# Graph network, kernel for one core: softmax weights and x1 are split into float16 halves before they are transposed, and the halves are transposed by DMA

## What is computed

```python
x = _layernorm(x + _L0_gnn_ref(x, adj, ...))     # two layers of graph attention
x = _layernorm(x + _L1_gnn_ref(x, adj, adj, ...))

# L0, for l in 0, 1
u = (u_left * (upper triangle and diagonal) + u_right * (lower triangle)) of adj   # u_* = h (h W_*)^T / sqrt(384)
delta = exp(u) * adj
h = relu(layer_norm(delta / (sum(delta) + 1e-10) @ (h W_lin^T + b_lin)) )

# L1, 12 heads of 32
scores = q k^T * 384 ** -0.5 + 2 * adj
p = softmax(scores), rows that are all zero give 0
out = (p @ v) W_o^T + b_o
```

## Time and profile before

| | |
|---|---|
| median of 3 runs | 2787.72 us |
| profiled execution | 2789.46 us |
| its span, first to last instruction | 2787.6 us |
| mean granted clock of TensorE | 0.992 of full speed |
| busy: PE, DVE, ACT, POOL | 98%, 85%, 66%, 53% |
| 16 DMA engines, queue of SP | 11.6% |

### The profile page before, as it was taken

One profiled execution on the slowest core, in us unless ns is written; L12 is line 12 of the kernel. 1 busy time (PEld: TensorE's weight loads), 2 busy tenths in 40 slices (PEclk: granted clock), 3 DMA queues, 4 the chain that ended last, 5 costly groups with the idle time before them and its releaser, 6 DMA issues.

```text
span 2787.6 us, 74097 instructions
## 1 busy us (share of the span) xinstructions
PE 2736.2 (98%) x27072; PEld 1766.4 (63%) x27072; DVE 2375.9 (85%) x8170; ACT 1846.2 (66%) x4363; POOL 1472.2 (53%) x1558
## 2 busy tenths in 40 slices
PE   6999999999999999999999999999999999999996
PEld 3666666666666666666666666666666666666664
DVE  4788988889888889888888888898888898888986
ACT  4666676666776666766666766667666667666665
POOL 2555464455555554654555554556545556445553
PEclk9999999999999999999999999999999999999998
DMA  4001101011101011010111010111011110101000
GB/s 169 23 34 49 46 22 46 34 49 46 49 22 46 35 49 46 25 43 35 49 49 46 22 46 35 49 46 37 31 37 46 49 46 22 46 35 49 25 28 18
DMA packets 55993, 116.68 MB, mean 42 GB/s; under 512 B 4945, under 2 KB 37713, under 8 KB 55633
## 3 DMA queue, kind: packets, MB, share of 16 engines
q1 hardware_dynamic: 55632, 111.96, 11.6%
HBM read 86.77 MB, written 25.17 MB: 40 GB/s over the span
## 4 chain that ended last, share of the span: by engine, by line
PE 97%; DVE 1%; issue 1%; ACT 0%; DMA 0%; POOL 0%; SPq 0%; POOLq 0%; DVEq 0%; ACTq 0%
PE psum L1243 72%; PE psum L1253 11%; PE psum L1307 7%; PE psum L1402 4%; PE psum L1376 3%; DMA s<-weights 0%; DVE s L837 0%; DVE y L900 0%; DVE st L962 0%; DVE z L1014 0%; DVE st L908 0%; DVE o L881 0%; DVE pT_lo L802 0%; ACT w L583 0%; DVE z L1023 0%
## 5 line engine op out<-in xcount | busy, mean ns | idle before, releaser
L583 ACT ACTIVATE w<-s,nmax 128x128 f32<-128x128 f32 x1536 | 480.6, 393 | 2.4 <-DVE nmax L837 2.4
L1243 PE MATMUL psum<-hT_hi,w_hi 128*128 128x512 f16 x1152 | 439.3, 381 | 12.1 <-POOL hT_lo L378 11.9
L459 POOL TENSOR_TENSOR fold<-s 128x768 f32<-128x768 f32 x128 | 242.2, 1892 | 387.5 <-DVE nmax L837 285.5
L1243 PE MATMUL psum<-hT_hi,w_lo 128*128 128x512 f16 x1152 | 438.1, 380 | 0.0
L1243 PE MATMUL psum<-hT_lo,w_hi 128*128 128x512 f16 x1152 | 438.1, 380 | 0.0
L523 ACT ACTIVATE nT_hi<-psum 128x512 f16<-128x512 f32 x384 | 227.5, 594 | 300.1 <-PE psum L1243 298.1
L837 DVE CUSTOM_DVE_ANT_0 s<-psum,adj 128x128 f32<-128x128 f32 x1536 | 339.4, 285 | 6.1 <-DVE live L857 0.5
L386 POOL TENSOR_TENSOR hl_lo<-hl_raw,hl_hi 128x384 fp32r<-128x384 f32 x256 | 238.6, 952 | 103.5 <-ACT hl_hi L523 99.2
L804 DVE SCALAR_TENSOR_TENSOR nT_lo<-psum,nT_hi 128x512 f16<-128x512 f32 x384 | 258.3, 683 | 31.0 <-ACT nT_hi L523 31.0
L802 DVE TENSOR_TENSOR pT_lo<-psum,pT_hi 128x512 f16<-128x512 f32 x384 | 251.2, 683 | 25.9 <-ACT pT_hi L523 25.5
L523 ACT ACTIVATE pT_hi<-psum 128x512 f16<-128x512 f32 x384 | 214.6, 594 | 81.4 <-PE psum L1253 80.6
(11 more groups left out here) (135 smaller groups left out, 7942.0 us busy)
## 6 DMA issues: line engine op xcount, KB each, us to landing
xTin<-xT SPq DMA_DIRECT2D x32, 768.0 KB, 4.8
xres<-x SPq DMA_DIRECT2D x32, 768.0 KB, 4.4
out<-y SPq DMA_DIRECT2D x128, 192.0 KB, 1.9
adjm<-adjM SPq DMA_DIRECT2D x32, 384.0 KB, 5.4
adjT_sb<-adjT SPq DMA_DIRECT2D x32, 256.0 KB, 5.5
adj<-adj SPq DMA_DIRECT2D x32, 256.0 KB, 2.8
x<-weights SPq DMA_DIRECT2D x4, 576.0 KB, 4.6
s<-weights SPq DMA_DIRECT2D x3, 576.0 KB, 6.4
```

Source lines behind the costliest of these rows:

```text
L459: nc.gpsimd.tensor_tensor(fold[:, :, 0:n], src[:, :, 0:n], src[:, :, n:2 * n], ALU.add)\
L583: last = nc.scalar.activation(w[:, m], s[b % 2][:, m], ACT.Exp, bias=nmax[b % 2][:, m:m + 1], scale=-1.0)
L1243: last = mm(dst, a, b, start=(i == 0), stop=(i == total - 1))
```

## The change

1. x1 and w are split where they lie, in the layout of tokens by features. ACT writes x1_hi (4 copies of 384) and p_hi (3 copies of 512 per graph). DVE writes x1_lo and two of three parts of p_lo, POOL the third. x1_hi and x1_lo lie in the buffer of xTin, p_hi and p_lo in the buffer s of the same graph.
2. PE's transposes x1t and pt are gone. SP issues `dma_start_transpose` for each half: two for x1 (turn_x) and two for each graph's weights (turn_p), ten a pass, of 128 x 1536 float16 each.
3. Waits: qk(0) and v(0) wait for both transfers of x1, pv(b) for both of its graph; DVE's scores(b, 0) waits until the transfers that read the same s are done; ACT's exps wait for pt_lo and pt_end (POOL's part) in place of PE; the load of the next xTin waits for the transfers of x1; out_bias on POOL waits for x1_lo.
4. xT_hi and xT_lo are laid out graph first.
5. All orders are new: BANK_USES, and `body` of SP, POOL, ACT, DVE and PE. Among them: PE does ctx(0, 0) and ctx(0, 1) ahead of qk(0); u(0) ahead of hl(0, 2); DVE does x1's low halves ahead of u(0, 0); xt(0) to xt(2) follow qk(3) on ACT; pv(1), pv(2) and v(3) come later.

The core of the diff:

```diff
-        xT_hi, xT_lo = (sb(f"xT_{p}", [KB, GROUP, TOK], f16) for p in ("hi", "lo"))
+        xT_hi, xT_lo = (sb(f"xT_{p}", [GROUP, KB, TOK], f16) for p in ("hi", "lo"))
...
+        def halves(buf, n):
+
+            all16 = buf.bitcast(f16)
+            return [all16[:, h * n:(h + 1) * n] for h in range(2)]
+
+        x1_hi, x1_lo = halves(xTin[:].rearrange("p k b t -> p (k b t)"), GROUP * FEAT)
+        p_hi, p_lo = zip(*(halves(b[:].rearrange("p h t -> p (h t)"), HEADS * TOK) for b in s))
...
+            def turn_x(p):
+
+                if not p.l1:
+                    return
+                if p.before.l1:
+                    sp.wait_ge(qk_full.sem, p.before.upto(qk_full, 2 * KB))
+                    sp.wait_ge(v_full.sem, p.before.upto(v_full, GROUP))
+                for ok, src, dst in ((x1t_hi, x1_hi, xT_hi), (x1t_lo, x1_lo, xT_lo)):
+                    sp.wait_ge(ok.sem, p.upto(ok, GROUP))
+                    sp.dma_start_transpose(dst[:].rearrange("p b k t -> p (b k) t"), src).then_inc(xT_in.sem, 16)
+
+            def turn_p(p, b):
+
+                if not p.l1:
+                    return
+                if b >= 2:
+                    sp.wait_ge(pv_full.sem, p.upto(pv_full, b - 1))
+                elif p.before.l1:
+                    sp.wait_ge(pv_full.sem, p.before.upto(pv_full, b + 3))
+                sp.wait_ge(pt_hi.sem, p.upto(pt_hi, KB * (b + 1)))
+                sp.dma_start_transpose(pT_hi[b % 2][:], p_hi[b % 2]).then_inc(pT_in[b % 2].sem, 16)
+                sp.wait_ge(pt_lo.sem, p.upto(pt_lo, 2 * (b + 1)))
+                sp.wait_ge(pt_end.sem, p.upto(pt_end, b + 1))
+                sp.dma_start_transpose(pT_lo[b % 2][:], p_lo[b % 2]).then_inc(pT_in[b % 2].sem, 16)
...
+                turn_x(p)
+                load_adj(p)
+                load_x(p)
+                load_adjT(p)
+                load_tri(p)
+                store(p, 2)
+                turn_p(p, 0)
+                turn_p(p, 1)
+                store(p, 3)
+                load_res(p)
+                turn_p(p, 2)
+                store(p, 0)
+                turn_p(p, 3)
+                store(p, 1)
...
+            def pt(p, b, r):
+
+                if not p.l1:
+                    return
+                pool.wait_ge(p_ok.sem, p.upto(p_ok, TILES * (b + 1)))
+                pool.wait_ge(pt_hi.sem, p.upto(pt_hi, KB * b + r + 1))
+                part = slice(TILES * r * TOK, TILES * (r + 1) * TOK)
+                nc.gpsimd.tensor_tensor(p_lo[b % 2][:, part], w[:].rearrange("p h t -> p (h t)")[:, part],
+                                        p_hi[b % 2][:, part], ALU.subtract).then_inc(pt_end.sem, 1)
...
             def pt(p, b, r):
                 if not p.l1:
                     return
...
-                hi(p, pt_full, KB * b + r, "pt", pT_hi[b % 2][:, TILES * r:TILES * (r + 1)], pt_hi)
+                act.wait_ge(fold1.sem, p.upto(fold1, b + 1))
+                act.wait_ge(p_ok.sem, p.upto(p_ok, TILES * b + r + 2))
+                part = slice(TILES * r * TOK, TILES * (r + 1) * TOK)
+                copy(p_hi[b % 2][:, part], w[:].rearrange("p h t -> p (h t)")[:, part]).then_inc(pt_hi.sem, 1)
...
+                of, n = (p, b - 2) if b >= 2 else (p.before, b + 2)
+                if j == 0 and of.l1:
+                    dve.wait_ge(live_ok.sem, of.upto(live_ok, n + 1))
+                    dve.wait_ge(pT_in[b % 2].sem, of.upto(pT_in[b % 2], 32 * (n // 2 + 1)))
...
-            def pt(p, b, r):
-
-                if not p.l1:
-                    return
-                n = KB * b + r
-                p.await_bank(pe, "pt", n)
-                pe.wait_ge(p_ok.sem, p.upto(p_ok, TILES * b + r + 2))
-                turn("pt", n, [w[:, TILES * r + i] for i in range(TILES)], pt_full)
-
...
-                pe.wait_ge(pt_lo.sem, p.upto(pt_lo, (b + 1) * KB))
+                pe.wait_ge(pT_in[b % 2].sem, p.upto(pT_in[b % 2], 32 * (b // 2 + 1)))
```

More of the change, by code:

```diff
@@ L299, in store @@
                     .then_inc(out_st[b % 2].sem, 16)
-            def body(p):
[L302 to L328, removed]
@@ new lines, in load_adj, with load_x @@
+            def load_adj(p):
+                if not p.l1:
+                    return
+                if p.before.l1:
+                    sp.wait_ge(s_ok.sem, p.before.upto(s_ok, GROUP * TILES))
+                sp.dma_start(adj2[:], adj[bass.ds(p.it - 1, 1)].rearrange("g i b j -> i (g b) j"))\
+                    .then_inc(adj2_in.sem, 16)
+            def load_x(p):
+                if not p.nxt:
+                    return
+                sp.wait_ge(xt_hi.sem, xt_hi.upto(p.it, KB))
+                sp.wait_ge(xt_lo.sem, xt_lo.upto(p.it, KB))
+                if p.l1:
+                    sp.wait_ge(xT_in.sem, p.upto(xT_in, 32))
+                sp.dma_start(xTin[:], xT[bass.ds(p.it + 1, 1)].rearrange("g p k b t -> p (g k) b t"))\
+                    .then_inc(x_in.sem, 16)
@@ new lines, in load_tri, with load_adjT @@
+            def load_tri(p):
+                if not p.nxt:
+                    return
+                sp.wait_ge(mask_ok.sem, mask_ok.upto(p.it, 1))
+                sp.dma_start(adjm[:], adjM[bass.ds(p.it + 1, 1)].rearrange("g j b c -> j (g b) c"))\
+                    .then_inc(adj_in.sem, 16)
+            def load_adjT(p):
+                if not p.nxt:
+                    return
+                if p.before.l0:
+                    sp.wait_ge(e_ok[1].sem, p.before.upto(e_ok[1], 2))
+                sp.dma_start(adjT_sb[:, 1 - p.odd], adjT[bass.ds(p.it + 1, 1)].rearrange("g j b i -> j (g b) i"))\
+                    .then_inc(adjT_in.sem, 16)
@@ L700, in body @@
                 ctx(p, 0, 3)
+                fin(p, 2)
+                qk(p, 0)
+                qk(p, 1)
                 qk(p, 2)
                 qk(p, 3)
+                fin(p, 3)
+                xt(p, 0)
+                xt(p, 1)
+                xt(p, 2)
                 qk(p, 4)
@@ L720, in body @@
                 nl(p, 1, 1)
-                v(p, 1)
+                exps(p, 1, 0)
                 exps(p, 1, 1)
-                nl(p, 1, 2)
                 exps(p, 1, 2)
-                v(p, 2)
+                pt(p, 1, 0)
+                setup(p, 8)
                 exps(p, 1, 3)
[L727 to L734, removed]
@@ L735, in body @@
-                fin(p, 3)
                 pt(p, 1, 1)
                 pt(p, 1, 2)
+                setup(p, 9)
+                hl(p, 1, 0)
+                v(p, 0)
+                v(p, 1)
                 exps(p, 2, 0)
+                nl(p, 1, 2)
+                nl(p, 1, 3)
+                v(p, 2)
                 exps(p, 2, 1)
                 exps(p, 2, 2)
+                exps(p, 2, 3)
+                pt(p, 2, 0)
+                pt(p, 2, 1)
+                to(p, 0)
+                hl(p, 1, 1)
@@ L1102, in body @@
                 resid(p, 3)
-                setup(p, 4)
-                y_bn(p, 1)
-                nl(p, 0, 4)
-                nl(p, 0, 5)
                 y_bn(p, 2)
@@ L1347, in qk @@
                 w = slice(kb * 128, (kb + 1) * 128)
-                product(bank("qk", c), [t for k in range(KB) for t in split(
-                    w_hi[:, 6 + part, k, w], w_lo[:, 6 + part, k, w],
-                    xT_hi[:, k].rearrange("p b t -> p (b t)"), xT_lo[:, k].rearrange("p b t -> p (b t)"))],
-                    qk_full, ready=(lambda k: pe.wait_ge(x1t_lo.sem, p.upto(x1t_lo, k + 1))) if c == 0 else None)
+                product(bank("qk", c).rearrange("p (b t) -> p b t", b=GROUP), [t for k in range(KB) for t in split(
+                    w_hi[:, 6 + part, k, w], w_lo[:, 6 + part, k, w], xT_hi[:, :, k], xT_lo[:, :, k])], qk_full)
             def v(p, b):
```

398 lines of the change are left out of this document (192 added, 206 removed).

## The result

The changed kernel takes **2750.51 us** (median of 4 runs, 2750.24 to 2752.05); the kernel before took 2787.82 beside it. The ratio is 0.9867, with an interval of 0.985 to 0.9884: 1.3% faster, where 4.7% were forecast (2656 us). The measured time lies in the stated range, but the gain is 37 us and not 132.

The account below looks back on a forecast made before the run. PE was taken to bound the kernel. Span 2787.6 minus 209 (transposes) plus 68 (stall) plus 9 (last groups) gave 2656, 2658 with 1.9 around it, and 2656 us as median; forecast range 2620 to 2700, wider range 2580 to 2850.

Parts of the forecast that it names:

- The direction: Whole kernel: faster than before, chance 0.64, against 0.06 for the same and 0.30 for slower.
- the removed part: PE's 60 transposes a pass, of weights and x1, go: 6.5 us a pass, 209 us in all.
- the 78.4 us a pass: PE's pass without transposes and without any other wait: 84.9 - 6.5 us.
- D: Transfer time of one 384 KB transposing transfer on SP, put at 1.5 us from plain transfers.
- f: Fixed part of the time a transfer on SP takes to land, put at 1.8 us from plain transfers.
- the 3.3 put: Time in us from issue to landing expected for one transposing xT or pT transfer on SP.
- The margins of 1.0 to 1.6 us: Time to spare at qk(0), pv(2) and scores(3) after a transfer pair lands, said to hide the transfers.
- (c): Rival: long transfers stall qk(0), pv(2) and scores(3) with pv(3), making the kernel slower, 2906 us at 3.5 us each; chance 0.24.
- (d): Rival: the transfer queue is the bound, ten transfers a pass at 10.0 us each, 3270 us; chance 0.06.
- The stall at ctx(0, 0): PE, ready at 23.4 us of the pass, waits for DVE's e_lo at 25.6: 2.2 us a pass.
- (b): Rival: DVE bound through contention with POOL, 12 new operations at their longest, 2720 us; chance 0.14, with smaller such losses.
- What is moved between engines: Low halves change form on DVE, copies and subtractions go to ACT and POOL; DVE keeps 74 us, 94% of the pass.

Follow-up runs that it names:

- stats64, experiment 8: The changed kernel with rs and nmr given one SBUF tensor input, plus all DVE statistics over 64 of 384 columns: 2673.29 us.
- plain_copy: The changed kernel with its ten transposing transfers a pass replaced by plain ones of the same bytes, so products get untransposed data: 2743.76 us.
- experiment 7: Four more statistics of 384 columns a pass on DVE: 2782.3 us added to the changed kernel, 2787.04 us added to the kernel before.
- experiment 2: The changed kernel with only rs given one SBUF tensor input, its reciprocal staying in PSUM: 2706.67 us.
- 6: The changed kernel with rs and nmr given one SBUF tensor input, plus plain transfers in place of the transposing ones: 2680.06 us.
- experiment 3: The changed kernel with DVE's fin(3) moved from behind den(0, 0) to behind qk(1): 2771.35 us.
- 4: The changed kernel with POOL's low halves of the next x waiting until DVE has normalised z: 2747.82 us.
- experiment 1: The changed kernel with DVE's small operations rs and nmr given only one tensor input in SBUF: 2703.45 us.
- one_pt22: The changed kernel with rs and nmr given one SBUF input, ACT's pt(2, 2) earlier, and SP's graph 3 transfers ahead of store(0): 2903.7 us.

## Why the prediction was right and wrong

**The direction and the removed part: right.** The transposes are gone (PE 2736.2 to 2581.7 us busy), and PE's own work is near the 78.4 us a pass that were put: in a pass of stats64 PE is busy for 78.8 of 80.7 us.

**The transfers: right in what they cost, though short in length.** D and f were taken from plain rows; one transfer takes 0.5 to 0.8 us longer than the 3.3 put, a pair 0.8. (A plain one of weights took 2.6, so the 3.3 were too long for a plain transfer and too short for a transposing one.) The margins of 1.0 to 1.6 us took that up; plain_copy shows 7 us for all of it. Rivals (c) and (d) fall.

**The stall at ctx(0, 0): wrong size.** e_lo was forecast at 25.6 us of the pass and ended at 24.8 (1433.91, with the pass's first product at 1409.10). PE was forecast there at 23.4 and came at 24.6, since it had waited 1.2 us for DVE's nT_lo on the way. So the stall is 0.3 us, and not because that chain was short: another wait had taken part of it over. The one term that the sum put on top of PE's 78.4 us was mostly not there, and the waits that were there had no term. That the forecast was not lower still is luck: a stall that did not come stood in for a part of DVE's waits. The measured time lies where the prediction put 0.14, for (b) or smaller losses of that kind up to 2782.

**The step that failed** is in "What is moved between engines": "So DVE keeps 74 us, 94% of a 78.4 us pass". The 74 us are right (2356.8 / 32 = 73.7), and then the sum treats an engine at 94% as one that never holds another: outside ctx(0, 0) it puts PE's waits for DVE at nothing. They are 2.4 us a pass of idle time on PE, and the pass is 83.18 us and not 78.4 + 0.3. It walked DVE's list at two places, x1 and softmax, and nowhere asked what it does to nT_lo, o and y, for which PE waits in each pass. The dose of experiment 7 is that step's test: the same four operations a pass cost nothing before and 32 us after.

**The port was priced at the wrong operations.** The prediction had the row of the contention and applied it to the 12 new subtractions of 0.7 us. They are hardly touched: the eight of the weights have a mean of 691 ns and the four of x1 553. What is touched are small products that did not change at all: rs, 172 ns in the median, up to 1810. The price of such an operation is not a share of its own length but what is left of POOL's instruction. The new orders put rs(0) right behind scores(2, 3), whose last maxima also start POOL's sum of s, and rs(1) right behind the start of a later step of a sum. That is 2.3 us a pass on DVE, and 44 us in the time (experiment 2), half of the 94 us that were missed. Rival (b) had the mechanism, DVE as bound through contention, at 2720; its place was wrong.

**The rest:** DVE's list without the port is worth some 30 us (experiment 8), and the transposing 23 once DVE is relieved (6), 5 of them in the tail. These were each taken from 2703, and not both at once, so they need not add up. The idle time ahead of nmr, which the profile seemed to show as a cost, could not be won (3). z's delay looked like 0.9 us a pass in the one pass that was read, and is 3.5 us in the whole run (4).

**The version of experiment 1 is faster than both kernels:** 2703.45 us, 3.1% under before.

## What to carry to other kernels

When the engine that sets the time gets lighter by 8%, walk the list of the next one to the end; an engine at 94% of the new pass stands in the way long before it is full. An operation of a few elements with two inputs in SBUF can cost what the other engine's longest instruction costs: compare the median with the maximum of its row, and give it an input in PSUM or as a scalar. Before a duration from one pass is multiplied by the number of passes, look at its row over the whole run: z took 2.5 us or more in 3 passes of 32. An idle time on an engine is worth its length only if what it does next isn't waiting for something else as well. A shift of 0.1 us can bring two operations together that had just missed each other, as in experiment 3. And a transfer moved on SP moves every store behind it.

## What the runs showed of the hardware

- A small DVE product with two SBUF inputs that starts just behind an instruction of POOL ends with it: 0.17 us become 1.81 beside a sum of 1.81 that started 0.04 us earlier; with one input in SBUF and one in PSUM all 128 take 0.17.
- One tensor input is not enough in every form: z<-z,rstd,nmr reads one tensor and two scalars, all in SBUF, and four of them took 2.56 us in place of 1.65 beside POOL's hT_lo (fin_late).
- A transposing transfer of 128 x 1536 float16 lands 3.8 to 4.1 us after issue and holds SP for a median of 1.4 to 1.8 us; a plain one of the same bytes lands after 2.6 to 3.4 us and holds it for 0.47 (plain_copy).
- After 4.6 us without a product the granted clock was 0.50 for 5.5 us (one_pt22); in the changed kernel's passes, with waits of up to 0.7 us, it stayed at 1.00.
